# Attention rebuilt: stationary values in three rounded passes, heads projected in pairs, output projection in the feed-forward kernel

## The reference, cut to what matters

```python
q, k, v = (x @ W for W in (Wq, Wk, Wv))          # [B, T, H, D]
q, k = rmsnorm(q) * q_rms_w, rmsnorm(k) * k_rms_w
gate = softplus(einsum('bthd,hd->bht', k, u / norm(u)) / 8)
bias = -dist(i, j) * (softplus(omega) * slopes)[h] * gate[b, h, j]   # causal: -inf for j > i
attn = softmax(q @ k.T / 8 + bias)
x = layernorm(x + (attn @ v) @ Wproj)
h = silu(x @ w1 * s1) * (x @ w2 * s2)            # hidden 1024
h = gelu(gelu(h @ h1 * s) @ h2 * s)
x = layernorm(x + h @ w3 * s3)
```

## Time and profile before

| what | value |
|---|---|
| median of 3 runs | 3853.31 us (3852.98 to 3854.8) |
| profiled execution, its own time | 3856.38 us |
| its span, first to last instruction | 3854.6 us |
| mean granted TensorE clock | 0.986 |
| PE busy | 3626.2 us, 94% |
| weight load busy | 3256.8 us, 84% |
| DVE busy | 1904.9 us, 49% |
| ACT busy | 1408.5 us, 37% |
| POOL busy | 469.5 us, 12% |

### The profile page before, as it was taken

One profiled execution on the slowest core, in us unless ns is written; L12 is line 12 of the kernel. 1 busy time (PEld: TensorE's weight loads), 2 busy tenths in 40 slices (PEclk: granted clock), 3 DMA queues, 4 the chain that ended last, 5 costly groups with the idle time before them and its releaser, 6 DMA issues. The chain is left out here.

```text
span 3854.6 us, 58589 instructions
## 1 busy us (share of the span) xinstructions
PE 3626.2 (94%) x24112; PEld 3256.8 (84%) x24112; DVE 1904.9 (49%) x3885; ACT 1408.5 (37%) x2367; POOL 469.5 (12%) x289
## 2 busy tenths in 40 slices
PE   3799999999999999999999999999899999989999
PEld 2698988989898898889889898898778888778887
DVE  3555566555665655666555566556233122132232
ACT  1244344444444444444444444444333232232222
POOL 3111211111211111121111211111000000000000
PEclk9899999999999999999999999999989999999999
DMA  1110001110001112000111000110121111130110
GB/s 54 34 26 19 21 19 23 30 27 21 20 21 23 44 28 69 21 20 21 29 25 26 20 21 20 26 28 21 32 98 41 52 47 47 38 136 33 66 66 17
DMA packets 116121, 137.69 MB, mean 36 GB/s; under 512 B 39568, under 2 KB 72464, under 8 KB 115856
## 3 DMA queue, kind: packets, MB, share of 16 engines
q1 hardware_dynamic: 115856, 133.96, 12.8%
HBM read 54.22 MB, written 29.36 MB: 22 GB/s over the span
## 5 line engine op out<-in xcount | busy, mean ns | idle before, releaser
L762 PEld LDWEIGHTS ps_v<-values,exps 128*128 128x128 f32 x8704 | 1129.9, 192 | 135.2 <-ACT exps L477 58.0
L762 PE MATMUL ps_v<-values,exps 128*128 128x65 f32 x8704 | 1146.8, 271 | 37.2 <-DVE y_tok L680 34.9
L477 ACT ACTIVATE exps<-ps_s,bias 128x512 f32<-128x512 f32 (+3 forms) x1280 | 797.5, 623 | 889.7 <-PE ps_s L750 570.3
L662 DVE TENSOR_REDUCE maxes<-ps_m 128x1 f32<-128x512 f32 (+3 forms) x1280 | 774.8, 609 | 598.0 <-PE ps_m L799 321.6
L799 PE MATMUL ps_m<-k_ext,q_max 128*128 128x512 f32 (+3 forms) x1280 | 546.3, 434 | 53.0 <-DVE maxes L662 52.6
L749 PE MATMUL ps_s<-q_twice,k_split 128*128 128x512 f32 (+3 forms) x1280 | 505.2, 395 | 0.0
L750 PE MATMUL ps_s<-q_ext,k_ext 128*128 128x512 f32 (+3 forms) x1280 | 469.9, 367 | 0.0
L725 PE MATMUL ps_p<-w_hi,xt_hi 128*128 128x194 f32 x1024 | 295.4, 288 | 25.5 <-POOL w_lo L410 20.4
L799 PEld LDWEIGHTS ps_m<-k_ext,q_max 128*128 128x128 f32 x1280 | 248.0, 194 | 73.5 <-issue 43.6
L487 ACT ACTIVATE raw<-ps_p 128x386 f32<-128x386 f32 x256 | 126.4, 494 | 445.5 <-PE ps_p L725 445.5
L725 PE MATMUL ps_p<-w_hi,xt_lo 128*128 128x194 f32 x1024 | 285.9, 279 | 0.0
(11 more groups left out here) (186 smaller groups left out, 5336.9 us busy)
## 6 DMA issues: line engine op xcount, KB each, us to landing
q_twice<-q_max SPq DMA_DIRECT2D x256, 128.0 KB, 2.3
k_split<-k_ext SPq DMA_DIRECT2D x128, 128.0 KB, 2.2
hidden<-gelu SPq DMA_DIRECT2D x64, 256.0 KB, 2.0
a_in<-hidden SPq DMA_DIRECT2D x8, 2048.0 KB, 10.3
x_rows<-in_L_attn_x_dram SPq DMA_DIRECT2D x16, 256.0 KB, 2.9
acc<-in_L_attn_x_dram SPq DMA_DIRECT2D x2, 2048.0 KB, 10.0
attended<-acc SPq DMA_DIRECT2D x8, 512.0 KB, 2.9
x_tok<-attended SPq DMA_DIRECT2D x8, 512.0 KB, 4.0
```

Of the source, the lines that this page charges most:

```text
L477: nc.scalar.activation(exps[:, u_ % PR, off:QB], ps_s[u_ % 2][:, off:QB], ACT.Exp, bias=bias[slot][:, kt, qb:qb + 1]).then_inc(ex_done, 1)
L662: nc.vector.tensor_reduce(maxes[:, qt, kc:kc + 1], ps_m[v % 2][:, 0:width], AX.X, ALU.max).then_inc(mx_free, 1)
L762: last = nc.tensor.matmul(ps_v[:, t * (D + 1):(t + 1) * (D + 1)], exps[:, u_ % PR, t * P:(t + 1) * P], values[second][:, kt, :], start=(kt ...
```

## The change

The planner `segment_steps` gives way to `attention_steps`, one list for all heads, whose due times are in heads and whose preparation is for a pair of heads:

```diff
+    for p in range(PAIRS):
+        t0 = 2.0 * p
+        at(t0 - 2.40, "weights", p)
+        for t in range(TT):
+            at(t0 - 1.68 + 0.036 * t, "project", p, t)
+        for i in range(4):
+            at(t0 - 1.09 + 0.05 * i, "square", p, i)
+        at(t0 - 0.90, "mean", p)
+        for i in range(4):
+            at(t0 - 0.89 + 0.04 * i, "power", p, i)
+        at(t0 - 0.74, "gate a", p)
+        for i in range(4):
+            at(t0 - 0.71 + 0.02 * i, "norm", p, i)
+        for i in range(GATE_PARTS):
+            at(t0 - 0.64 + 0.01 * i, "gate b", p, i)
+        for s in range(2):
+            n = 2 * p + s
+            first = t0 - 0.53 if s == 0 else t0 + 0.015
+            at(first + 0.01, "values in", n, 0)
+            at(first + 0.06, "values in", n, 1)
+            turns = [first + 0.005 + 0.033 * i for i in range(NTURN)]
+            start, end = (turns[1] + 0.03, t0 + 0.28) if s == 0 else (t0 + 0.29, t0 + 1.29)
```

```diff
-                        for t in range(max(0, kt - TQ * qb), TQ):
-                            last = nc.tensor.matmul(ps_v[:, t * (D + 1):(t + 1) * (D + 1)],
-                                                    exps[:, u_ % PR, t * P:(t + 1) * P], values[second][:, kt, :], ...
+                    pe.wait_ge(hi_done, u_ + 1)
+                    nc.tensor.matmul(bank[:, off:QB], v_main[s][:, kt, :], e_hi[:, u_ % S_RING, off:QB], ...
+                    nc.tensor.matmul(bank[0:VCOLS, off:QB], v_rest[s][:, kt, :], e_hi[:, u_ % S_RING, off:QB], ...
+                    pe.wait_ge(lo_done, u_ + 1)
+                    nc.tensor.matmul(bank[:, off:QB], v_main[s][:, kt, :], e_lo[:, u_ % S_RING, off:QB], ...
```

```diff
+                    nc.scalar.activation(e_hi[:, u_ % S_RING, off:QB], ps_s[u_ % 2][:, off:QB], ACT.Exp, bias=by).then_inc(hi_done, 1)
+                    if u_ >= E_RING:
+                        act.wait_ge(lo_done, u_ + 1 - E_RING)
+                    nc.scalar.activation(e_all[:, u_ % E_RING, off:QB], ps_s[u_ % 2][:, off:QB], ACT.Exp, bias=by).then_inc(ex_done, 1)
```

```diff
+                if step[0] == "scores":
+                    gp.wait_ge(hi_done, u_ + 1)
+                    gp.wait_ge(ex_done, u_ + 1)
+                    if u_ >= S_RING:
+                        gp.wait_ge(pv_done, u_ + 1 - S_RING)
+                    nc.gpsimd.tensor_tensor(e_lo[:, u_ % S_RING, off:QB], e_all[:, u_ % E_RING, off:QB],
+                                            e_hi[:, u_ % S_RING, off:QB].bitcast(F32), ALU.subtract).then_inc(lo_done, 1)
```

```diff
-                        nc.vector.reciprocal(recip[:], pv[:, :, D]).then_inc(rc_done, 1)
+                    nc.vector.reciprocal(recip[:], ps_v[grp % 2][D:P, :]).then_inc(rc_done, 1)
+                    nc.vector.tensor_tensor(y_out[:, grp % 2, :], ps_v[grp % 2][0:D, :], recip[:], ALU.mult).then_inc(y_done, 1)
```

Projection: 392 columns of two heads in one matmul, single bank, copied by ACT tile by tile; squares, powers and norms are four each per pair. The turns of a pair's first head wait for the whole gate chain:

```diff
+                    pe.wait_ge(pj_free, TT * p + t)
+                        last = nc.tensor.matmul(ps_p[:, 0:WCOLS], a, c, start=i == 0, stop=i == len(terms) - 1)
+                    nc.gpsimd.tensor_tensor(sq[:, i % 2, :, :], raw[:, :, col:col + D], raw[:, :, col:col + D], ALU.mult).then_inc(sq_done, 1)
+                    nc.gpsimd.tensor_tensor(rs[:, i, :], mean_sq[:, i, :], power[:], ALU.pow).then_inc(rs_done, 1)
+                    glink(nc.vector.tensor_tensor(raw[:, :, col:col + D], raw[:, :, col:col + D],
+                                                  rs[:, i, :].unsqueeze(2).broadcast_to([P, TT, D]), ALU.mult))
+                if step[0] == "turn":
+                    if i == 0:
+                        pe.wait_ge(gate, GATE * (n // 2 + 1))
```

`ffn_up` reads `yt` and x, and projects before it normalises; ps_1 is the accumulator, the transposes move from chunk 3 to chunk `TURN` = 6:

```diff
+            def project_y(i, c):
+                pe.wait_ge(ylo_done, m + 1)
+                for t in range(NT):
+                    for j, (y, w) in enumerate(((y_hi, wp_hi), (y_hi, wp_lo), (y_lo, wp_hi))):
+                        last = nc.tensor.matmul(out, y[:, m % 2, tok], w[:, c, :], ...
+                last.then_inc(y_used, 1)
...
                 for o in range(OC):
-                    if o == 3 and more:
+                    if o < OC // 2 and more:
+                        project_y(i + 1, 2 * o)
+                        project_y(i + 1, 2 * o + 1)
+                    if o == TURN and more:
                         turn_x(i + 1)
```

More of the change, by code:

```diff
@@ L103, in segment_steps @@
-    for u in range(LEAD if main else NU, NU + LEAD):
-        tile("scores", u)
-        tile("values", u - LAG)
-        qb, kt = UNITS[(u - LAG) % NU]
-        if main and u - LAG < NU and kt == TQ * (qb + 1) - 1:
-            steps.append(("divide", qb))
-            if odd:
-                outs += [(u + 1 + i, ("out", qb, i)) for i in range(NYM)]
-        done += length[u % NU]
-        while outs and outs[0][0] <= u:
-            steps.append(outs.pop(0)[1])
-        while main and extra and (extra[0][0] * sum(length) <= done or u == NU + LEAD - 1):
-            steps.append(extra.pop(0)[1])
@@ L116, in segment_steps, with at @@
-    assert not outs
+    def at(when, *step):
+        extra.append((when, len(extra), step))
+    for j in range(NXT):
+        at(-9.0 + 0.01 * j, "x", 0, j)
+        at(H - 3.1 + 0.16 * j, "x", 1, j)
+    for p in range(PAIRS):
+        t0 = 2.0 * p
+        at(t0 - 2.60, "load", p)
+        at(t0 - 2.40, "weights", p)
[7 more added lines that the diff above has]
+        at(t0 - 0.74, "gate a", p)
+        at(t0 - 0.72, "gate exp", p)
+        for i in range(4):
[5 more added lines that the diff above has]
+            first = t0 - 0.53 if s == 0 else t0 + 0.015
+            at(first, "bias", n)
+            at(first + 0.01, "values in", n, 0)
+            at(first + 0.06, "values in", n, 1)
+            turns = [first + 0.005 + 0.033 * i for i in range(NTURN)]
+            for i, when in enumerate(turns):
+                at(when, "turn", n, i)
+            start, end = (turns[1] + 0.03, t0 + 0.28) if s == 0 else (t0 + 0.29, t0 + 1.29)
+            for v, (qt, kc) in enumerate(MAXES):
+                qb = qt // TQ
+                when = max(start + (end - start) * v / (NM - 1), turns[2 * qb + 1] + 0.03)
+                at(when, "max", n, v)
+                if v + 1 == maxes_to(qb):
+                    at(when + 0.001, "most", n, qb)
+                    at(when + 0.03, "shift", n, qb)
@@ new lines, in attention_steps, with extras @@
+    extra.sort()
+    steps, done, twice, turned = [], 0, 0, set()
+    def extras(until):
+        while extra and extra[0][0] <= until:
+            step = extra.pop(0)[2]
+            steps.append(step)
+            if step[0] == "turn":
+                turned.add(step)
+    extras(0.0)
+    length = [min(TQ, TQ * (qb + 1) - kt) for qb, kt in UNITS]
+    for u in range(HEADS * NU + LAG):
+        if u < HEADS * NU:
+            n, v = divmod(u, NU)
+            qb, kt = UNITS[v]
+            g = n * NQB + qb
+            if kt == 0:
+                while twice < min(g + Q_RING, HEADS * NQB) and ("turn", twice // NQB, 2 * (twice % NQB) + 1) in turned:
+                    steps.append(("twice", *divmod(twice, NQB)))
+                    twice += 1
+                assert twice > g
+            steps.append(("scores", n, v))
+            done += length[v]
+        if u >= LAG:
+            n, v = divmod(u - LAG, NU)
+            qb, kt = UNITS[v]
+            steps.append(("values", n, v))
+            if kt == TQ * (qb + 1) - 1:
+                steps.append(("divide", n, qb))
+        extras(done / sum(length))
@@ L350, in _ @@
+            for i in range(2):
+                sp.wait_ge(y_out_done[i], 16 * HEADS * NQB // 2)
         @block.gpsimd
@@ L951, in sp_body @@
                 load_x(sp, i + 1)
+                for c in range(OC - 1):
+                    load_y(sp, i + 1, c)
             for o in range(OC):
-                if more and o == 3:
+                if more and o == 1:
+                    load_y(sp, i + 1, OC - 1)
+                if more and o == TURN:
                     store_x1(sp, i + 1)
```

1125 lines of the change are left out of this document (553 added, 572 removed).

## The result

The changed kernel takes 4307.36 us (median, 4306.06 to 4315.44) where the kernel before takes 3854.06: a ratio of 1.118 with an interval of 1.1161 to 1.12. The forecast was 3983, its range ended at 4120. The sign was right, the size was not: +453 where +130 was forecast.

What follows compares the result with a forecast made beforehand. PE bounds the kernel; the change saves it 36 us a pair, but POOL and DVE take it back: 167 us for 165.4. With start, last pair and ffn_up, +130 on 3856.4 gives 3986, median 3983; range 3775 to 4120.

Steps and rivals of the forecast that it cites:

- take for each stretch the engine with the most work: Attention: a pair of heads cut by due times, each stretch lasting as its busiest engine; 165.5 us, 167 with turns.
- From 0 to 0.29: First stretch of a pair, in heads: DVE sets it with 23.4 us (two divides, turns, maxima), PE 19.3.
- From 0.90 to 1.25: Stretch of a pair, in heads: POOL sets it with 34.6 us (subtractions 15.7, squares 7.6, powers 11.6), PE 18.
- From 1.25 to the first turn: Gate stretch, 1.25 to 1.47 heads: DVE sets it with 24.7 us, a divide and waits for POOL included; PE 9.5.
- From the first turn to 1.80: Stretch from 1.47 heads: POOL sets it with 22.8 us (subtractions, values in, weights), plus 1.5 for turns.
- Rival 3: Attention: close engines with hand-overs and PE below full clock make 175 to 180 us a pair, 4105 to 4180; chance 0.24.
- Rival 1: Attention: reciprocal of 512 costs 0.69 us, nobody waits for the port; 155.7 us a pair, 3816, 1% faster; chance 0.30.
- POOL's load: Attention: subtractions at 1.29 us for 512 columns, squares, powers, values in and weights sum to 121 us a pair before waits.
- Rings allow no more: Attention: with in-order queues and values lagging two units, POOL's or DVE's surplus in one stretch isn't made up in another.
- The last pair: Attention's last pair, without projection, squares or powers: 105 to 110 us where 138 stood before, -30.
- The start: Before attention: DVE constants to about 67 us, then 16 projections of 3 us, gate and turns; first scores 171 for 158, +13.
- `ffn_up`: Blocks 1 to 7: project_y's 96 matmuls 11.36 us and a new PE wait of 3.6 before them; 7 x 15 = +105.

Runs made afterwards that it cites:

- e7: Changed kernel with the division moved out of attention: one reciprocal of all sums in ffn_up, each chunk of y multiplied by it; 4065.38 us.
- e2: Changed kernel with POOL's four powers a pair replaced by products of the same tiles, the root left out; 4171.52 us.
- v3: v1 with the weights' rounded copy on ACT and POOL's four powers a pair replaced by products, the root left out; 3722.32 us.
- r1: Changed kernel with one more buffer of e_hi and e_lo and the value matmuls three units behind the scores, not two; 4253.1 us.
- e5: Changed kernel with some 50 unread matmuls a pair just where PE stands: ahead of gates, first shift and third maximum behind a divide; 4295.73 us.
- e3: Changed kernel with 70 unread matmuls of 512 columns more a pair, among squares, powers, norms and gate steps; 4321.4 us.
- v1: Changed kernel with division in ffn_up, squares and value copies on ACT, later project_y and turns, r1's edit, DVE's constant rows behind the first weights; 3876.59 us.

## Why the prediction was wrong

**The step that failed** is "take for each stretch the engine with the most work", for DVE's divides. In the forecast a divide is 4.2 us of DVE's work and costs time only where DVE has the most: by its own numbers the eight of a pair are worth some 8 us (from 0 to 0.29 DVE's 23.4 against PE's 19.3, and 4.2 before the first turn). e7 gives 17.0 for them, though a copy of 0.68 us is left of each. A divide stops PE as well, and PE's own work comes behind it: the time is nearer to a sum than to a maximum.

- From 0 to 0.29 the forecast had DVE at 23.4; DVE is in fact busy for 22.9, yet the stretch lasts 30.5: PE, with 24.6 of its own at the lower clock, stands for 5.9, of which 4.6 are waits for maxima behind two divides, and DVE in turn waits for PE's next maxima. With the divides gone (e7) the maximum nearly holds again, 23.0 for PE's 21.3.
- From 0.90 to 1.25 the match (35.9 for 34.6) is luck. POOL was busy for 31.3, not 34.6, and two divides held PE and POOL up. In e7 the stretch takes 31.8 for POOL's 31.1: with the powers and squares in it, and no divides, the maximum holds.
- From 1.25 to the first turn the forecast had one chain, the gates, with the divide in it, and was near (25.7 for 24.7): it begins 3 us late, behind the last power, and has fewer waits for POOL than were costed.
- From the first turn to 1.80 it had POOL with 22.8 and 1.5 for the turns. POOL is busy for 17.7 of the 32.0; PE is the busiest with 25.2, and stands for 6.8, of which 5.2 behind the divide. e7 takes 28.5 there with PE at 25.3.

From 0.29 to 0.90 (48.8 for 49.0) and from 1.80 to 2.0 (11.5 for 11.0) PE is busy throughout and the forecast held. The size of the divide was in the forecast (3.5 us, measured 3.36); that PE would stop behind it was not. The powers (2.91 us) are no part of the failure: the forecast had their 11.6 us on the path whole, and e2 gives 8.2 a pair for them, v3 10.0.

**Rival 3** named the coupling and the clock and had 175 to 180 us a pair; it was the nearest (184.3), though short of it, and its chance of 0.24 looks too low. Of its two halves the coupling is shown by e7 and r1. Of the clock e5 gave back 1.1 us a pair in the mean and 3.3 in the best pair. PE is busy for 148.5 us of a pair where 129 were forecast; that most of the excess lies where PE would wait anyway is argued from e3 and e5, not shown.

**Rival 1** took the divide for short. The reciprocal takes 3.36 us, 6.6 ns an element, so the difference of two rows gave it within 5%. The Trainium skill's repeat count of 8 (VectorE: DVE Perf Modes, "First, the fixed hardware budget"), which made 4.3 by the forecast's own estimate, is over a quarter too long here; the measurement decides.

**POOL's load** was right: 120.7 us a pair for 121, 1.314 for the subtraction's 1.29. The mutual waiting of POOL and DVE is there and was put too high: the norms take 1.71 us in the mean and 1.21 alone, 0.5 more as costed, but of the small instructions only five of a pair are held for long. From the groups' means all of it comes to some 6.5 us a pair (an estimate), where 9 were in the sum. "Rings allow no more" was right too, and r1 prices it: one unit more is worth 54 us while the divides are there.

**The last pair** (-30 forecast, +1 measured) missed twice. Its base was too long by 10: before, it takes 127.6 us to the last divide and not 138, since the 15 pairs ahead of it take 166.1 in the mean and not 165.4. And it fell to the same step: the forecast counted PE's work alone, 105 to 110, where it takes 127.0 to its last scores, 30.5 of it in the first stretch as in any other pair. In e7 it takes 109.4.

**The start** (+13, measured +34): the constants on DVE end at 75 us and not at 67, and the first projection stands 4 us behind them. The 16 projections take 46.0 as forecast (48). Squares, powers, norms and gates, with nothing beside them, take 34.8 from the last projection to the first turn; the forecast left 56 for these and the turns, and they took 67.5. v1, which moves the constants, took 34 us back.

**`ffn_up`** (105 for blocks 1 to 7, measured 120): the wait (3.55 for 3.6) and the matmuls (11.5 for 11.4) were right. The 1.9 us a block at half the clock behind the wait were missed, though the same was seen at the start. Block 0 with attention's end came to 18, as forecast.

What stays open: the 28.5 us that e7 still takes between the first turn and 1.80, where the forecast had 24.3. PE has 25.3 of work there at a mean clock of 0.86, and stands for 3.2; no run took the lower clock, the chain of turns or the waits for POOL away alone. Nor was ACT's own ring (`E_RING`, two tiles) made deeper.

## What to carry to other kernels

When queues are in order and only two tiles lie between engines, the divide of this case (4 us on DVE) had to be added in good part to PE's work, which waits for the same queue: 17 us a pair for 25 of DVE's time. The maximum over engines held where one engine was busy throughout, and in the powers' stretch once the divides were gone. Before moving work to an idle engine, find the longest single instruction that it brings, what is queued behind it and the chain that waits for its result; busy shares of 51% and 45% hid both. Here the change was worth having with the divide taken once for all sums, the root on DVE with the gates right behind it, squares on ACT, and the smaller edits of v1: 3764.76 for 3854 before and 4307 as it was made.
